# Stack rows six partitions apart, a reordered start-up, and expert weights spread over seven samples

## The chip, the cores and the metric

One core of a Trainium2 chip. The metric is the device time of one launch in microseconds (us). TensorE is PE, VectorE is DVE, ScalarE is ACT, GpSimd is POOL, SyncE is SP. SPq, ACTq and POOLq are the same engines where they issue DMAs.

## What is computed

Sixteen samples of 333 rows x 256 columns (256 image rows, 77 text rows) go through one attention block and one mixture-of-experts block. Cut to what matters:

```python
h = concat([clip(|diagonal difference| + |anti-diagonal difference|, 0, 1), table[x_txt]])   # 16 x 333 x 256
n = layernorm(h); q, k, v = n@Wq+bq, n@Wk+bk, n@Wv+bv                  # 16 heads of 16 columns
# windows of 128 rows, stride 64, and one last window: 5 windows a sample
scores = q_win @ k_win.T / 4 + pos_bias; o = softmax(scores) @ v_win    # added up, divided by the count
h = h + (merged @ Wo + bo)
# feed-forward: top 2 of 8 experts by softmax(layernorm(h) @ gate_w.T), each silu(x@w1)*(x@w3)@w2
h = h + weighted sum of the two experts
```

## The kernel before, in words

**Two phases.** First an attention phase, a software pipeline over samples. Every engine runs `step(b)` for b = -3 to 17 (L291), and each step has 20 slots k (5 windows x 4 head groups). In step b, sample b is in attention (`att`), sample b+1 is projected to q, k and v (`proj`), sample b+2 has its layernorm (`inp`), sample b+3 has its image differences (`pre`), sample b-1 is finished (`tail`) and sample b-2 is sorted to its experts (`tail2`). Then an expert phase: 91 tiles of 128 gathered rows, all on PE (L1206 to L1245).

**The order of work is written out by hand.** Each engine executes its own program in order and waits on semaphores; a DMA queue's issue order is the order of the code of SP, ACT or POOL. Nothing is planned or reordered by a tool.

**q and k in three bf16 parts.** To compute float32-like scores in bf16, q and k are split into three parts: part 0 is a bf16 copy (DVE, L757), the rest is formed on POOL (L508), part 1 is a bf16 copy of the rest (DVE, L764), part 2 what is left (POOL, L516). Scores need six products of parts, and each head has 16 columns, so the contraction is stacked to 6 x 16 = 96 rows. `Q_SLOTS = (0, 1, 2, 0, 1, 0)` and `K_SLOTS = (0, 0, 0, 1, 1, 2)` say which part stands in which of the six slots. The parts reach this layout through DRAM: SP writes each part (`write_part`, L363, two DMAs of 83.2 KB each) and loads it back once for each slot that uses it (`load_stack`, L369, one DMA of 166.5 KB for each slot, 16 partitions of 333 x 16 bf16 values). Per sample that is 12 write DMAs and 12 load DMAs. Slot s takes partitions 16s to 16s+15. PE waits for all 12 loads at the first slot of the sample (`stack_in`, L1061) and contracts over partitions 0 to 95 (L1066).

**SP's order in a step** (L334 to L403): the image loads of sample b+3 and its text indices, the positional bias in step -1 (L351, 1 MB), then for sample b+1 the writes and loads of parts mixed with each other, each load behind a wait for the write of its part (`parts_out`, L370), then the shifted copies of v (L397 to L401). The weights (`load_weights`, L317) go out in step -2.

**POOL's start-up** (L442 to L470): memsets of the image buffers, constants (`const_set` counts them to 11), both `h_in` buffers, all of `v_all` (3840 columns), the pad rows, and two DMAs of pad rows. Then its steps: the gather of the text rows in slot 0 of step b for sample b+2 (L536), the differences in slot 12 or 15 (L567), the inverse roots in slot 13 (L482 to L491), the residual in slot 18 (L598).

**DVE** waits for `zeroed` (L725) before its steps. In a step it does the max over scores plus bias (L783), the layernorm sums (L730), the normalisation (L738), the absolute values of the differences (L902), and in step 0 the negation of the bias (L750), which the first L783 needs.

**ACT** waits for `prep_done` (L629), which DVE sets when it has scaled `bq_col` (L747), and starts with the copy of xT (L639). In step 0 it issues the w1 and w3 of experts 0 to 6 in slots 2, 4, ... 14 (L668 to L672), 14 DMAs of 512 KB. The weights of expert 7 and all w2 come after the last sample (L408 to L417), since their place is used by other buffers until then.

Of the kernel before, what the change touches and what calls it, by code (L numbers as in the profile page):

```python
# [18 lines left out]
ACT = mybir.ActivationFunctionType  # L19
AX = mybir.AxisListType  # L20

P = 128
B, IMG, D = 16, 256, 256
TXT = 77
# [35 lines left out]
def build(nc, x, x_txt, table, Wq, bq, Wk, bk, Wv, bv, Wo, bo, pos_bias, gate_wT, w1, w2, w3, use, out):  # L60
    ctx = ExitStack()
    with ctx:
# [133 lines left out]
        zeroed = sem("zeroed")  # L196
        x_zeroed = sem("x_zeroed")
# [32 lines left out]
        pv_done = sem("pv_done")  # L230
        raw_ready = sem("raw_ready")
# [84 lines left out]
        def _(sp):  # L316
# [17 lines left out]
            def step(b, par):  # L334
                att, tail, tail2, proj, inp, pre = has(b)
                b0, b1, b3 = b - 1, b + 1, b + 3
                if b == -2:
                    load_weights()
                if pre:
# [10 lines left out]
                if b == -1:  # L350
                    sp.dma_start(nbias[:, :, :], pos_bias.rearrange("h q k -> q h k")).then_inc(bias_in, 16)  # L351
# [8 lines left out]
                if proj:  # L360
# [32 lines left out]
                    load_stack(1, 2, k_stack[par1], K_SLOTS)  # L393
                    vt = v_win[par1]
# [46 lines left out]
        def _(pool):  # L441
            pool.memset(x_here[:, :, :], 0.0).then_inc(x_zeroed, 1)  # L442
            pool.memset(x_below[:, :, :], 0.0).then_inc(x_zeroed, 1)
            pool.memset(text_idx[:, :], 0).then_inc(x_zeroed, 1)
            pool.memset(ident[:, :], 0.0).then_inc(const_set, 1)
# [23 lines left out]
            pool.dma_start(slots_dram[E * REGION:E * REGION + P, :], pad_rows[:, :]).then_inc(pads_in, 16)  # L469
            pool.dma_start(out[TOKENS:TOKENS + P, :], pad_rows[:, 0:D]).then_inc(pads_in, 16)  # L470
# [21 lines left out]

            def step(b, par):
                att, tail, tail2, proj, inp, pre = has(b)
                b9, b0, b1, b2, b3 = b - 2, b - 1, b + 1, b + 2, b + 3

# [22 lines left out]
                for k in range(G):  # L519
# [11 lines left out]
                    if inp and k == 0:  # L531
                        pool.wait_ge(idx_in, b2 * 16 + 16)
                        if b2 >= 2:
                            pool.wait_ge(res_ready, b2 - 1)
                            pool.wait_ge(xn_ready, b2 * 3 - 3)
                        pool.indirect_dma_start(h_in[par][0:TXT, 2, :], None, table,  # L536
                                                bass.IndirectOffsetOnAxis(text_idx[0:TXT, 0:1], 0)).then_inc(text_in, 16)
# [90 lines left out]
        def _(act):  # L628
            act.wait_ge(prep_done, 1)  # L629

            def step(b, par):
                att, tail, tail2, proj, inp, pre = has(b)
                b9, b0, b1 = b - 2, b - 1, b + 1
                for k in range(G):
# [33 lines left out]
                    if b == 0 and k >= 2 and k % 2 == 0 and k // 2 < E:  # L668

                        e = k // 2 - 1  # L670
                        act.dma_start(w1_sb[:, e], w1[e].rearrange("(c p) n -> p c n", p=P)).then_inc(expert_weights_in, 16)
                        act.dma_start(w3_sb[:, e], w3[e].rearrange("(c p) n -> p c n", p=P)).then_inc(expert_weights_in, 16)  # L672
# [41 lines left out]
        def _(dve):  # L714
# [10 lines left out]
            dve.wait_ge(zeroed, 5)  # L725
# [15 lines left out]
            def step(b, par):  # L741
# [33 lines left out]
                for k in range(G):  # L775
# [59 lines left out]
                    if tail2 and k == 3:  # L835

                        dve.wait_ge(score_e_ready, b9 + 1)
                        if b9 >= 1:
# [59 lines left out]
                    if pre and k == (13 if b > -2 else 17):  # L898
# [4 lines left out]
                    if proj and k == 14:  # L903
# [379 lines left out]
```

## Time and profile before

| | |
|---|---|
| median of 3 runs | 1293.54 us (1292.12 to 1294.58) |
| the profiled execution | 1295.08 us, span 1293.2 us |
| PE, DVE, ACT, POOL busy | 89%, 65%, 55%, 46% of the span |
| DMA | 123.31 MB, mean 95 GB/s |

The page gives busy shares over the whole span, which mixes a start-up, the attention phase (to about 750 us) and the expert phase. The view by stretches of time separates them, and the view of waits says what ended the idle time of an engine. The rows are further down.

### The profile page before, as it was taken

Reading aid. Unit: us, or ns where it says so; the run is one execution under the profiler, and the core shown is the slowest. Engines: PE = TensorE matmul, PEld = TensorE weight load, DVE = VectorE, ACT = ScalarE, POOL = GpSimd, SP = SyncE. Lnnn points to the kernel's source line nnn. Section 1 sums busy time; section 2 is a strip of 40 time slices with the busy share of each in tenths; the row PEclk is TensorE's granted clock in tenths of the full one; section 3 lists DMA queues with packets and bytes.
Section 4 is the critical chain, followed back from the end, with each engine's and each line's share of the span. In section 5 each row is a group of like instructions: output and inputs, shape, how many; then the busy total and the mean of one; then the engine's idle time right before and its main releaser. Section 6 shows DMA issues by size and latency. Waiting matters only on the chain. (4 is left out here: it accounts for less than half of the span.)

```text
span 1293.2 us, 34357 instructions
## 1 busy us (share of the span) xinstructions
PE 1154.7 (89%) x10510; PEld 950.5 (73%) x10511; DVE 839.2 (65%) x4259; ACT 707.9 (55%) x1976; POOL 595.2 (46%) x750
## 2 busy tenths in 40 slices
PE   1385999999999999999998729999999999999996
PEld 0263767666676676666766419999999999999995
DVE  4372999899899998989887643444444444444442
ACT  0194999999999999999998601111111111111110
POOL 6551576566665676656653432332223332223332
PEclk9697999999999999999998859999999999999998
DMA  3794665457554675556642171223323223323322
GB/s 103 159 254 108 133 130 116 109 134 153 123 110 108 141 157 109 109 120 130 141 95 67 35 244 29 48 48 49 49 45 49 46 48 49 49 45 49 49 46 32
DMA packets 98394, 123.31 MB, mean 95 GB/s; under 512 B 15544, under 2 KB 87416, under 8 KB 95192
## 3 DMA queue, kind: packets, MB, share of 16 engines
q1 hardware_dynamic: 75880, 89.96, 30.8%
q0 software_dynamic: 18576, 24.47, 11.8%
q10 hardware_dynamic: 3808, 7.34, 2.0%
q8 instruction: 59, 0.97, 0.4%
q14 instruction: 71, 0.58, 0.2%
HBM read 69.35 MB, written 46.07 MB: 89 GB/s over the span
## 5 line engine op out<-in xcount | busy, mean ns | idle before, releaser
L666 ACT ACTIVATE probs<-probs,neg_max 128x128 f32<-128x128 f32 x1280 | 402.3, 397 | 1.9 <-DVE neg_max L783 1.5
L783 DVE CUSTOM_DVE_ANT_0 probs<-s_bank,nbias 128x128 f32<-128x128 f32 x1280 | 293.9, 285 | 87.4 <-PE s_bank L1066 80.5
L705 ACT ACTIVATE v_all<-s_bank 128x512 f32<-128x512 f32 x91 | 54.4, 598 | 285.9 <-PE s_bank L1222 265.9
L1077 PE MATMUL t_bank<-ident,probs 128*128 128x128 f32 x1280 | 195.8, 276 | 0.2 <-ACT probs L666 0.2
L1237 PE MATMUL o_bank<-stacks,v_all 128*128 x728 | 172.4, 380 | 0.3 <-issue 0.2
L659 ACT ACTIVATE probsT<-t_bank 128x512 f32<-128x512 f32 x240 | 142.2, 592 | 42.1 <-PE t_bank L1077 40.1
L618 POOL DMA_INDIRECT out_dram<-wq_sb,nbias x46 | 75.8, 1649 | 193.2 <-DVE wq_sb L987 179.9
L1066 PE MATMUL s_bank<-stacks 96*128 96x128 bf16 x1280 | 127.3, 222 | 37.9 <-DMA stacks<-qk_parts 37.8
L1066 PEld LDWEIGHTS s_bank<-stacks 96*128 96x128 bf16 x1280 | 94.5, 99 | 82.0 <-DMA stacks<-qk_parts 40.1
L618 POOL DMA_INDIRECT out_dram<-wk_sb,nbias x45 | 73.5, 1634 | 175.8 <-DVE wk_sb L987 172.8
L993 DVE TENSOR_TENSOR v_all<-v_all,t_bank 128x512 f32<-128x512 f32 x91 | 62.6, 688 | 129.8 <-PE t_bank L1222 129.8
L1237 PEld LDWEIGHTS o_bank<-stacks,v_all 128*128 128x128 f32 x728 | 131.3, 190 | 15.1 <-issue 0.9
L1093 PE MATMUL o_bank<-probsT,v_all 128*32 128x128 f32 x2560 | 137.0, 286 | 5.8 <-ACT probsT L659 3.4
L1077 PEld LDWEIGHTS t_bank<-ident,probs 128*128 128x128 f32 x1280 | 135.9, 142 | 0.9 <-ACT probs L666 0.5
L499 POOL DMA_INDIRECT expert_slots<-rows,slot_i x96 | 97.2, 1012 | 45.2 <-issue 36.7
L699 ACT ACTIVATE v_all<-m_bank 128x256 f32<-128x256 f32 x91 | 35.0, 384 | 143.6 <-PE m_bank L1211 143.6
L783 DVE DVE_READ_ACCUMULATOR2_ANT neg_max<- 128x1 f32 x1280 | 104.8, 82 | 0.0
L1093 PEld LDWEIGHTS o_bank<-probsT,v_all 128*32 128x32 f32 x2560 | 50.5, 108 | 61.8 <-issue 47.0
L1222 PEld LDWEIGHTS s_bank<-v_all,probs 128*128 128x128 f32 x736 | 91.0, 195 | 3.2 <-ACT v_all L699 0.9
L1222 PE MATMUL s_bank<-v_all,probs 128*128 128x128 f32 x736 | 91.4, 278 | 0.5 <-ACT v_all L699 0.5
L1222 PE MATMUL t_bank<-v_all,probs 128*128 128x128 f32 x736 | 90.4, 276 | 0.0
L1222 PEld LDWEIGHTS s_bank<-v_all,parts_flat 128*128 128x128 f32 x720 | 87.4, 192 | 3.0 <-ACT v_all L699 0.7
(159 smaller groups left out, 2002.3 us busy)
## 6 DMA issues: line engine op xcount, KB each, us to landing
stacks<-qk_parts SPq DMA_DIRECT2D x192, 166.5 KB
qk_parts<-parts_flat SPq DMA_DIRECT2D x192, 83.2 KB
nbias<-expert_slots SPq DMA_DIRECT2D x91, 129.0 KB
w_sb<-in_L_ffn_w_dram ACTq DMA_DIRECT2D x14, 512.0 KB
v_all<-v_all SPq DMA_DIRECT2D x64, 96.0 KB
x_here<-in_x_dram SPq DMA_DIRECT2D x16, 256.0 KB
out_dram<-h_res SPq DMA_DIRECT2D x16, 256.0 KB
stacks<-in_L_ffn_w_dram SPq DMA_DIRECT2D x8, 512.0 KB
```

What stands on the lines that cost most here:

```text
L499: pool.indirect_dma_start(slots_dram[:, :], bass.IndirectOffsetOnAxis(slot_i[0:n, kk, j:j + 1], 0), rows[0:n, kk, j, :], None).then_inc(sc ...
L618: pool.indirect_dma_start(out[:, :], bass.IndirectOffsetOnAxis(g_rows[r][:, D + 1:D + 2].bitcast(I32), 0), y_sb[r], None, compute_op=ALU.a ...
L659: act.activation(probsT[:, r, :], t_bank[:, r, :], ACT.Copy).then_inc(pT_by_act, 1)
L666: ins = act.activation(seg, seg, ACT.Exp, bias=neg_max[:, r, i:i + 1], scale=-1.0)
L705: act.activation(hidT[r % 2], s_bank[:, r % 2, :], ACT.Silu).then_inc(silu_ready, 1)
L783: ins = dve.tensor_tensor_reduce(probs[:, r, i * WIN:(i + 1) * WIN], s_bank[:, k % 2, i * WIN:(i + 1) * WIN], nbias[:, h, :], 1.0, BIG, AL ...
L993: dve.tensor_tensor(hidT[r % 2], hidT[r % 2], t_bank[:, r % 2, :], ALU.mult).then_inc(hid_ready, 1)
L1066: mm = pe.matmul(s_bank[:, k % 2, i * WIN:(i + 1) * WIN], q_stack[par][0:KROWS, h, lo:lo + WIN], k_stack[par][0:KROWS, h, lo:lo + WIN], st ...
L1077: mm = pe.transpose(t_bank[:, (k - 3) % 2, i * WIN:(i + 1) * WIN], probs[:, r, i * WIN:(i + 1) * WIN], ident[:, :])
L1093: mm = pe.matmul(o_bank[32 * i:32 * i + 32, vp, g * WIN:(g + 1) * WIN], v_win[bp][:, w, c0:c0 + 2 * HD], probsT[:, (k - 4) % 2, i * WIN:(i ...
L1222: mm = pe.matmul(bank[:, par, n * P:(n + 1) * P], up_w[par][:, m, a, n * P:(n + 1) * P], gxT[par][:, a * P:(a + 1) * P], start=(a == 0), s ...
L1237: mm = pe.matmul(o_bank[:, r % 2, 0:D], hidT[r % 2][:, a * P:(a + 1) * P], w2_sb[:, bass.ds(e, 1), a, :].rearrange("p o n -> p (o n)"), st ...
```

## The change

It does six things.

1. `load_stack` writes slot s to partitions s, s+6, s+12, ... s+90 in place of 16s to 16s+15, for q and k alike. PE still contracts over partitions 0 to 95 of both, so each row of q still meets its row of k.
2. For sample 0 alone, SP's order is another: all writes but for two waits stand ahead of most loads.
3. The positional bias is loaded in step -2, behind the weights, in place of step -1.
4. POOL's start-up is cut up: `h_in` is zeroed first; `v_all` is filled in two halves, in steps -3 and -1; the pad rows come in slot 10 of step -1; the text gather of sample 0 goes to slot 0 of step -3. The differences of sample 1 go to slot 17 of step -2 and wait for the normalised rows of sample 0.
5. ACT runs one Exp on a constant before it waits for `prep_done`.
6. ACT issues w1[b] in slot 0 and w3[b] in slot 2 of each step b from 0 to 6, one expert for each step.

```diff
 SP, step b:
                 if b == -2:
                     load_weights()
+                    sp.dma_start(nbias[:, :, :], pos_bias.rearrange("h q k -> q h k")).then_inc(bias_in, 16)
...
-                if b == -1:
-                    sp.dma_start(nbias[:, :, :], pos_bias.rearrange("h q k -> q h k")).then_inc(bias_in, 16)
...
-                                sp.dma_start(dst[s * HD:(s + 1) * HD, :, :], parts_dram[n, part, :, :, :])\
+                                sp.dma_start(dst[s:KROWS:len(slots), :, :], parts_dram[n, part, :, :, :])\
                                     .then_inc(stack_in, 16)
-                    if b1 >= 1:
-                        sp.wait_ge(stack_in, b1 * STACK_IN)
+                    if b1 == 0:
+                        write_part(0, 0, part1_ready)
+                        write_part(1, 0, part1_ready)
+                        write_part(0, 1, part2_ready)
+                        load_stack(0, 0, q_stack[par1], Q_SLOTS)
+                        write_part(0, 2, part3_ready)
+                        write_part(1, 1, part2_ready)
+                        write_part(1, 2, part3_ready)
+                        load_stack(1, 0, k_stack[par1], K_SLOTS)
+                        for t in range(1, 3):
+                            load_stack(0, t, q_stack[par1], Q_SLOTS)
+                            load_stack(1, t, k_stack[par1], K_SLOTS)
+                if proj and b1 >= 1:
+                    sp.wait_ge(stack_in, b1 * STACK_IN)
 (the order of L378 to L393 stays for b1 >= 1)
 POOL:
+            for i in range(2):
+                pool.memset(h_in[i][:, :, :], 0.0).then_inc(h_zeroed, 1)
             pool.memset(ident[:, :], 0.0).then_inc(const_set, 1)
...
-            for i in range(2):
-                pool.memset(h_in[i][:, :, :], 0.0).then_inc(zeroed, 1)
-            pool.memset(v_all[:, :], 1.0).then_inc(zeroed, 1)
-            pool.memset(pad_rows[:, 0:D + 1], 0.0).then_inc(zeroed, 1)
-            pool.memset(rows[:, :, :, D:ROW], 0.0).then_inc(zeroed, 1)
-            pool.wait_ge(zeroed, 5)
-            pool.wait_ge(const2_set, 5)
-            (and the two DMAs of pad rows)
+            def fill_values(half):
+                n = NW * VCOLS
+                pool.memset(v_all[:, half * n:(half + 1) * n], 1.0).then_inc(v_filled, 1)
+            def fill_pads():
+                (the two memsets, wait_ge(zeroed, 2), wait_ge(const2_set, 5), the two DMAs)
...
+                    if b == -3 and k == 0:
+                        fill_values(0)
+                        pool.wait_ge(h_zeroed, 2)
+                        pool.wait_ge(idx_in, 16)
+                        gather(0)
+                    if b == -1 and k == 1:
+                        fill_values(1)
+                    if b == -1 and k == 10:
+                        fill_pads()
-                    if inp and k == 0:
+                    if inp and b2 >= 1 and k == 0:
...
-                    if pre and k == (12 if b > -2 else 15):
+                    if pre and k == (17 if b == -2 else 12):
                         pool.wait_ge(x_in, b3 * 64 + 64)
+                        if b == -2:
+                            pool.wait_ge(xn_ready, 3)
 ACT:
+            act.wait_ge(const_set, 11)
+            act.activation(raw[:, 0:P], ident[:, :], ACT.Exp).then_inc(table_loaded, 1)
+            act.wait_ge(table_loaded, 1)
             act.wait_ge(prep_done, 1)
...
-                    if b == 0 and k >= 2 and k % 2 == 0 and k // 2 < E:
-                        e = k // 2 - 1
-                        act.dma_start(w1_sb[:, e], ...); act.dma_start(w3_sb[:, e], ...)
+                    if 0 <= b < E - 1 and k in (0, 2):
+                        dst, src = ((w1_sb, w1), (w3_sb, w3))[k // 2]
+                        act.dma_start(dst[:, b], src[b].rearrange("(c p) n -> p c n", p=P)).then_inc(expert_weights_in, 16)
 DVE:
-            dve.wait_ge(zeroed, 5)
...
+                        if b9 == 0:
+                            dve.wait_ge(zeroed, 2)          (tail2, k == 3)
-                    if pre and k == (13 if b > -2 else 17):
+                    if pre and k == (17 if b == -2 else 13):
...
                     if proj and k == 14:
+                        if b1 == 0:
+                            dve.wait_ge(v_filled, 2)
```

## Rows read from the trace of the kernel before

**Rows 1.** Busy time by stretch: us, each engine (x instructions), PEclk, DMA share, GB/s.
```profile
40.00:60.00 20.00, 0.73 (x4) 0.30 (x2) 5.32 (x10) 0.00 (x0) 14.26 (x24) 0.63 0.87 155
...
100.00:120.00 20.00, 7.63 (x64) 5.86 (x65) 3.86 (x29) 5.00 (x14) 0.00 (x0) 0.58 0.55 122
120.00:140.00 20.00, 20.00 (x201) 13.91 (x200) 16.11 (x106) 18.56 (x55) 10.47 (x10) 1.00 0.43 77
...
200.00:240.00 40.00, 38.29 (x407) 27.70 (x410) 35.80 (x232) 37.46 (x111) 26.86 (x37) 1.00 0.57 129
...
840.00:880.00 40.00, 40.00 (x303) 38.43 (x302) 17.95 (x29) 7.26 (x15) 11.36 (x7) 1.00 0.32 50
```

**Rows 2.** PE timeline: start, us, line, out<-in, count [idle before, releaser].
```profile
26.58 1.34 PE L1122 MATMUL m_bank<-ident,xn 128*128 128x128 f32 x6 [26.58 <-DVE xn L738]
...
60.36 0.61 PE L1066 MATMUL s_bank<-stacks 96*128 96x128 bf16 x4 [19.63 <-DMA stacks<-qk_parts]
...
94.99 0.43 PE L1093 MATMUL o_bank<-probsT,v_all 128*32 128x128 f32 x8 [0.25 <-DVE probsT L792]
112.37 0.61 PE L1066 MATMUL s_bank<-stacks 96*128 96x128 bf16 x4 [16.96 <-DMA stacks<-qk_parts]
```

**Rows 3.** PE's waits between 200 and 700 us: us in total, times, longest.
```profile
PE m_bank L1179 <- DVE v_all L771: 7.7, 10, 1.0
...
PE s_bank L1066 <- DMA stacks<-qk_parts: 1.2, 2, 0.7
```

**Rows 4.** POOL timeline, start-up.
```profile
4.93 3.29 POOL L464 MEMSET v_all<- 128x3840 f32 x1
...
10.73 1.09 POOL L567 TENSOR_TENSOR diag<-x_here,x_below 128x512 f32<-128x512 f32 x1
...
15.75 1.07 POOL L536 DMA_INDIRECT h_in<-in_L_txt_weight_dram,text_idx  x1 [0.21 <-issue]
```

**Rows 5.** DVE timeline, start-up and first scores.
```profile
18.58 1.08 DVE L730 BATCH_NORM_STATS2 stats<-h_in 128x6 f32<-128x256 f32 x3 [5.08 <-DMA h_in<-in_L_txt_weight_dram,text_idx]
...
23.86 2.57 DVE L738 TENSOR_SCALAR xn<-h_in,moments,rstd 128x256 f32<-128x256 f32 x3 [3.99 <-POOL rstd L490]
...
50.97 1.22 DVE L750 TENSOR_SCALAR nbias<-nbias 128x2048 f32<-128x2048 f32 x1
61.13 0.29 DVE L783 CUSTOM_DVE_ANT_0 probs<-s_bank,nbias 128x128 f32<-128x128 f32 x1 [8.94 <-PE s_bank L1066]
```

**Rows 6.** ACT timeline, start-up.
```profile
28.02 1.28 ACT L639 ACT_TABLE_LOAD   x1 [28.02 <-PE m_bank L1122]
```

**Rows 7.** SP's issue timeline for sample 0.
```profile
36.04 3.64 SPq L366 DMA_DIRECT2D qk_parts<-parts_flat  x4
...
54.40 2.57 SPq L373 DMA_DIRECT2D stacks<-qk_parts  x3
```

**Rows 8.** DMA view, 42 to 43 us: packets by size; queue: packets, MB, share of 16 engines.
```profile
DMA packets 34, 0.18 MB, mean 181 GB/s; under 512 B 17, under 2 KB 17, under 8 KB 17
...
q1 hardware_dynamic: 34, 0.18, 121.8%
```

**Rows 9.** DMA view, 54 to 55 us (part writes alone, 666-byte packets).
```profile
q1 hardware_dynamic: 189, 0.12, 52.6%
```

**Rows 10.** DMA view, 66 to 67 us (ACT's weight loads, 2 KB packets).
```profile
DMA packets 197, 0.37 MB, mean 371 GB/s; under 512 B 16, under 2 KB 16, under 8 KB 197
```

**Rows 11.** SP's issue timeline for sample 1 (69 to 109 us).
```profile
76.29 2.37 SPq L373 DMA_DIRECT2D stacks<-qk_parts  x3
...
106.72 1.82 SPq L373 DMA_DIRECT2D stacks<-qk_parts  x3
```

**Rows 12.** SP's issue timeline for sample 2 (124 to 150 us).
```profile
132.23 1.35 SPq L373 DMA_DIRECT2D stacks<-qk_parts  x3
...
147.17 2.21 SPq L373 DMA_DIRECT2D stacks<-qk_parts  x3
```

**Rows 13.** DMA view, 85 to 90 us: ACT's queue, q10.
```profile
q10 hardware_dynamic: 611, 1.18, 82.8%
```

More of the change, by code:

```diff
@@ L196, in build @@
         zeroed = sem("zeroed")
+        h_zeroed = sem("h_zeroed")
+        v_filled = sem("v_filled")
         x_zeroed = sem("x_zeroed")
@@ L230, in build @@
         pv_done = sem("pv_done")
+        table_loaded = sem("table_loaded")
         raw_ready = sem("raw_ready")
@@ L393, in step @@
                     load_stack(1, 2, k_stack[par1], K_SLOTS)
+                if proj:
                     vt = v_win[par1]
@@ L461, in _ @@
                                base=TXT, pattern=[[0, 1]], channel_multiplier=-1).then_inc(const_set, 1)
-            for i in range(2):
-                pool.memset(h_in[i][:, :, :], 0.0).then_inc(zeroed, 1)
-            pool.memset(v_all[:, :], 1.0).then_inc(zeroed, 1)
-            pool.memset(pad_rows[:, 0:D + 1], 0.0).then_inc(zeroed, 1)
-            pool.memset(rows[:, :, :, D:ROW], 0.0).then_inc(zeroed, 1)
-            pool.wait_ge(zeroed, 5)
-            pool.wait_ge(const2_set, 5)
-            pool.dma_start(slots_dram[E * REGION:E * REGION + P, :], pad_rows[:, :]).then_inc(pads_in, 16)
-            pool.dma_start(out[TOKENS:TOKENS + P, :], pad_rows[:, 0:D]).then_inc(pads_in, 16)
             NEWTON = 3
@@ L491, in inverse_roots @@
                     ins.then_inc(root_step if i < NEWTON - 1 else rstd_ready, 1)
+            def fill_values(half):
+                n = NW * VCOLS
+                pool.memset(v_all[:, half * n:(half + 1) * n], 1.0).then_inc(v_filled, 1)
+            def fill_pads():
+                pool.memset(pad_rows[:, 0:D + 1], 0.0).then_inc(zeroed, 1)
+                pool.memset(rows[:, :, :, D:ROW], 0.0).then_inc(zeroed, 1)
+                pool.wait_ge(zeroed, 2)
+                pool.wait_ge(const2_set, 5)
+                pool.dma_start(slots_dram[E * REGION:E * REGION + P, :], pad_rows[:, :]).then_inc(pads_in, 16)
+                pool.dma_start(out[TOKENS:TOKENS + P, :], pad_rows[:, 0:D]).then_inc(pads_in, 16)
             def step(b, par):
@@ L495, in step, with gather @@
                 b9, b0, b1, b2, b3 = b - 2, b - 1, b + 1, b + 2, b + 3
+                def gather(n):
+                    pool.indirect_dma_start(h_in[n % 2][0:TXT, 2, :], None, table,
+                                            bass.IndirectOffsetOnAxis(text_idx[0:TXT, 0:1], 0)).then_inc(text_in, 16)
                 def scatter(kk, j):
@@ L535, in step @@
                             pool.wait_ge(xn_ready, b2 * 3 - 3)
-                        pool.indirect_dma_start(h_in[par][0:TXT, 2, :], None, table,
-                                                bass.IndirectOffsetOnAxis(text_idx[0:TXT, 0:1], 0)).then_inc(text_in, 16)
+                        gather(b2)
                     if att and k == 3:
@@ L667, in step @@
                         ins.then_inc(exp_ready, 1)
-                    if b == 0 and k >= 2 and k % 2 == 0 and k // 2 < E:
-                        e = k // 2 - 1
-                        act.dma_start(w1_sb[:, e], w1[e].rearrange("(c p) n -> p c n", p=P)).then_inc(expert_weights_in, 16)
-                        act.dma_start(w3_sb[:, e], w3[e].rearrange("(c p) n -> p c n", p=P)).then_inc(expert_weights_in, 16)
+                    if 0 <= b < E - 1 and k in (0, 2):
+                        dst, src = ((w1_sb, w1), (w3_sb, w3))[k // 2]
+                        act.dma_start(dst[:, b], src[b].rearrange("(c p) n -> p c n", p=P)).then_inc(expert_weights_in, 16)
                     v = (k - 4) // NG
@@ L837, in step @@
                         dve.wait_ge(score_e_ready, b9 + 1)
+                        if b9 == 0:
+                            dve.wait_ge(zeroed, 2)
                         if b9 >= 1:
```

## The prediction, made before the changed kernel was run

> **What bounds the kernel now.** I read the time by stretches first [rows 1]. From 200 us on, PE is busy 38.3 of 40 us, and in the expert phase 40 of 40, while DMA stands at 0.57 and 0.32. In two early stretches PE is nearly idle: 0.73 of 20 us from 40 to 60, and 7.6 of 20 from 100 to 120. So the kernel is bound by PE from about 112 us to its end, and what lies ahead of that is latency. PE's timeline names the holes [rows 2]. PE starts at 26.58, when the first normalised rows are there. Sample 0's scores start at 60.36 after 19.63 us of waiting for the stack loads. Sample 1's start at 112.37 after 16.96 us of the same wait, though PE had done sample 0's attention by 95.4. Between 200 and 700 us the same wait totals 1.2 us [rows 3]; PE's largest wait there, 7.7 us for v, is not touched by the change. Nothing behind 112 us is tied to a date of its own: samples follow each other (SP's first writes at 165.39, 206.56, 247.67: 41.1 us), then the tiles. Whatever the start gives back moves the end by as much.
>
> So there are three places: the path to PE's first work, the stack loads of sample 0, and those of sample 1.
>
> **Part 1, the path to the first work (POOL, ACT; changes 4 and 5).** Before, POOL fills all of v_all in 3.29 us, zeroes and writes the pads, and so reaches the first difference at 10.73 with no wait ahead of it; the text gather comes behind the image work, at 15.75, and DVE's sums wait 5.08 us for it, until 18.58 [rows 4, 5]. After, half the fill (1.65 us) and the gather's issue (1.07 us) stand ahead of the difference; a half fill and the pads leave. POOL's constants end at 3.64 before and at 5.1 with the two h_in memsets ahead of them. 5.1 + 1.65 + 1.07 makes 7.8, with some wait for the indices 8.1. From difference to clipped image took 4.8 us (10.73 to 15.54), so the image is there at 12.9; the gather, issued at about 7.1 and landing in 3 to 5 us, is no longer last. The sums start at 12.9 in place of 18.58, 5.7 us earlier. Sums 1.3 and roots 3.95 us keep their length. The normalisation took 2.57 us, since its first piece ran beside POOL's next difference; that difference now waits for it, so I take 3 x 0.405 less overlap, 1.1 us, from the later normalisations of the same form. The normalised rows come at 19.3 in place of 26.5. Behind that wait on POOL stand only the two differences of sample 1, and behind these DVE's absolute values and the scaling of bq_col, for which ACT waits: 19.5 + 2.1 + 0.4 + 0.2, so 22.3, 1.6 us later than PE's transposes end. ACT then copies xT without its table load of 1.28 us [rows 6]. xT is ready at 23.1 in place of 30.04: **7.0 us earlier**. The bias DMA, which stands ahead of sample 1's image on SP's queue, moves 1 MB; at the 0.37 MB for each us of [rows 10] that is 2.8 us, and puts that image at 19 to 20, about when it is asked for. If it is 2 us later, this term is 5.
>
> The second half fill and the pads (1.65 and some 1.8 us of POOL) lie in step -1. The first stands while PE projects q. The pads delay sample 1's layernorm, not sample 0's parts. Counted at nothing; without the cover the second would show in the next part.
>
> **Part 2, sample 0's stacks (changes 1, 2, 3).** Before, the first write goes out at 36.04, the last three loads from 54.40 to 56.97, and PE starts at 60.36 [rows 7]: 24.3 us. How much of that is data? Between 42 and 43 us 17 large packets of 10.7 KB (one row of a stack load) took 121.8% of 16 engine-us [rows 8]: 19.5 / 17 = 1.15 us each, 9 GB/s an engine. Each load puts one packet on each of 16 engines, so 12 loads are 13.8 us. A write is 8 packets an engine; 189 of them took 52.6% of 16 us [rows 9], 0.0445 us each, so 0.36 us. From the first large packet at 41.0 to the last at 58.3 that is 12 loads and 8 writes, 16.7 of 17.3 us. So this stretch was bound by DMA engines, and a mere reordering of SP's queue gains little.
>
> What a row six partitions further costs, no row shows. Bounds: 1.15 us again (sixteen neighbours or not is all the same), and at best the rate of the 2 KB packets, 371 / 16 = 23 GB/s, so 0.46 us [rows 10]. I take 0.6, near the fast end, since both sorts go from DRAM to SBUF over the same engines, and what sets the slow one apart is that all its rows land in sixteen neighbouring partitions. Worse than 1.15 isn't excluded and is a rival below.
> By the Trainium skill (SBUF — State Buffer, section Door 1: The DMA port swizzle) sixteen adjacent partitions reach four of 16 ports, and port use limits a DMA. Six apart, at most two rows of a load share a port, by which the packet would take half, an estimate of 0.57 us; the slow packets agree with it, and no row here tests the rest.
> Against it, the same page (The DMA setup-cost knee) has each DMA pay about 2 us whatever its size. Were that all, loads of 166.5 KB would gain nothing from their rows and the sum would be that of the first rival.
>
> Now the chain. With the parts 7.0 us earlier, part 0 of q is ready at 29.0, and part 2 of k, the last, at 36.6. SP: writes from 29.05, the last write ends at 38.8, the last load's issue at 42.6 (0.42 us each, and a wait for the last write of 2.5 us). At 0.6 us a packet the engines keep up with the issue: 42.6 + 1.05 to the first byte + 0.6 + 2.05 (58.3 to 60.36) is 46.3. At 1.15 us the data starts at 35 and takes 15.9 us: 52.9. The next to be late is DVE: sample 1's differences (POOL, 38.4, behind the pads), roots to 44.8, normalisation, then the bias at 45.9 to 47.1 (before 50.97 to 52.2, [rows 5]). So the first L783 runs at 47.6 in place of 61.13: **13.5 us earlier** (7.5 at the slow bound), part 1 included. The early bias also takes 1 MB out of the queue ahead of the first writes; that is in the 2.5 us of landing assumed here.
>
> **Part 3, sample 1's stacks (changes 1 and 6).** PE needed 35.0 us for sample 0 (60.36 to 95.4). The first three loads went out 15.9 us after its start, the last ones at 106.72, 30.4 us later [rows 11]; for sample 2 the same stretch was 14.9 us [rows 12]. The difference is ACT's seven experts: from 85 to 90 us its queue took 82.8% of the engines [rows 13], and each load waits for the landing of a write behind them. With one expert at slots 0 and 2, 1 MB, gone by about 6 us after the start, while the first write comes at 8.8 us, sample 1 has sample 2's chain: 15.9 + 14.9 + 2.2 for the last issues + 3.4 to land is 36.4 at the old packet, 1.4 beyond PE; with the faster packet each of the four waits for a write is over 1 us shorter, about 32, within PE's 35.0. The stall of 16.96 us goes: **17.0 us** (15.5 at the slow bound). The scores right after it took 0.61 us for four [rows 2] where those at full clock take 0.39; this cost of restarting PE, 0.58 of full clock in that stretch [rows 1], lasts for a few groups, 1 us at most, and I don't count it.
>
> **Part 4, the rest.** Six steps get two ACT DMA issues of 0.4 to 0.5 us; in step 0 fourteen such issues left ACT's activations back to back, nothing. Their 1 MB meets a stretch in which DMA stood at 0.43 [rows 1]. Faster packets in later samples free DMA, not PE. The expert phase is as before.
>
> **Sum.** 13.5 + 17.0 = 30.5 us. The span goes from 1293.2 to 1262.7, the profiled execution from 1295.08 to 1264.6. That execution is 1.5 us above the median, so the median goes to **1263.0**.
>
> **Rivals.** (a) *Rows make no difference to a packet.* Then 7.5 + 15.5 = 23 us, 1270.5. For it: DMA may be limited at the DRAM side or by latency. Against: the same engines carry 2.5 times as much in other transfers. It is also the case in which change 1 doesn't do what it says. 0.25. (b) *The spread weights meet stack loads that are just in time.* PE already waits for stacks twice, 1.2 us in all, between 200 and 700 us [rows 3], so some steps have no slack at the old packet. If 2.8 us of weights push the chain in each, 6 x 2.8 = 17 us comes back: 1280. Against: they are issued 12 us ahead of the first write. 0.07. (c) *Slower than before: rows six apart make each packet dearer.* It would be the stack loads of all samples. Since they are just in time, x us more for each of 12 loads costs 12x in each of 15 samples, 180x. From x = 0.17 (the 30.5 us above) it decides; at 1.5 us a packet, x = 0.35, it is 63 us on top of a start worth 23, 1333. Nothing in the trace speaks for it but that the shape doesn't occur. 0.03. The forecast's own case has 0.62; 0.03 is left for start-up waits that I haven't seen, to 1290.
>
> **How the numbers follow.** Forecast case: 1256 to 1268 from the packet at 0.46 to 0.8 and the part 1 term at 5 to 8.5. Adding (a) with 4 us for its own spread gives 1255 to 1275, which leaves (b), (c) and the remainder out, and a little of each side. A measurement tells 0.2%, 2.6 us, from no change. Faster by more: forecast, (a), (b) and most of the rest, 0.95. Within: 0.02. Slower: 0.03.
>
> **What the profile will show.** Right: PE's first transposes at 19 to 20; first L783 near 47.6; no wait for stacks at sample 1, whose scores start near 82; large packets near 0.6 us and DMA share from 200 us at 0.45 in place of 0.57; the step still 41.1 us. The forecast is wrong if the stack wait stays at either place over 3 us, if packets stay at 1.15 (then a), if steps 1 to 6 are longer than steps 8 to 13 (then b), or if all are (then c).

## The result and the profile after

The kernel takes **1264.09 us** (1263.12 to 1266.19), against 1294.06 us (1292.12 to 1296.04) for the kernel before in the same comparison. The ratio is 0.9771 [0.975, 0.9791], so 30.0 us or 2.3% faster. The forecast was 1263.0, for a gain of 30.5. The profiled execution took 1263.12 us, with a span of 1261.2 us against 1293.2.

The view by stretches comes first, in the columns of [rows 1] (stretch, length, then busy us of PE, PEld, DVE, ACT and POOL, the granted clock, DMA share, GB/s):

```profile
40.00:60.00 20.00, 10.09 (x71) 7.46 (x72) 10.03 (x58) 8.20 (x24) 11.05 (x21) 0.65 0.67 173
...
100.00:120.00 20.00, 19.68 (x209) 14.26 (x207) 19.36 (x119) 18.24 (x55) 12.48 (x23) 1.00 0.58 164
200.00:240.00 40.00, 38.77 (x412) 27.79 (x411) 36.38 (x234) 37.55 (x111) 25.99 (x35) 1.00 0.51 147
400.00:440.00 40.00, 38.77 (x413) 27.84 (x415) 36.51 (x236) 37.50 (x111) 25.78 (x37) 1.00 0.45 126
```

The second hole is gone: from 100 to 120 us PE is busy 19.68 us where it had 7.6. The first is shorter: 10.09 of the 20 us from 40 to 60, where it had 0.73. The steady stretches have the same PE work with less DMA time beside it. PE's timeline after (start, us, work, idle time before it and its releaser) answers to [rows 2]:

```profile
19.73 1.34 PE L1161 MATMUL m_bank<-ident,xn 128*128 128x128 f32 x6 [19.73 <-DVE xn L773]
...
49.91 0.61 PE L1105 MATMUL s_bank<-stacks 96*128 96x128 bf16 x4 [16.59 <-DMA stacks<-qk_parts]
...
84.38 0.40 PE L1105 MATMUL s_bank<-stacks 96*128 96x128 bf16 x4
```

Transposes start at 19.73 (26.58 before), sample 0's scores at 49.91 (60.36). The row at 84.38 is the first of sample 1's scores (112.37), and nothing stands in its brackets: no wait. PE's waits over 0 to 200 us name the stack loads once, where the view of before had both holes:

```profile
PE s_bank L1105 <- DMA stacks<-qk_parts: 16.6, 1, 16.6
```

To divide the gain I read three marks in each trace: the first scores of sample 0, SP's first write of a part for sample 2, and the first expert tile.

| mark, us | before | after | earlier by | gained since the mark above |
|---|---|---|---|---|
| first scores, sample 0 | 60.36 | 49.91 | 10.45 | 10.45, start-up and first stacks |
| first write, sample 2 | 124.47 | 95.57 | 28.90 | 18.45, the hole ahead of sample 1 |
| first expert tile | 772.85 | 740.96 | 31.89 | 3.0, steps between |
| span | 1293.2 | 1261.2 | 32.0 | 0.1, expert phase |

The forecast had 13.5, 17.0 and nothing.

**The start-up** came as the steps had it. POOL's timeline after, beside [rows 4]:

```profile
7.21 1.17 POOL L518 DMA_INDIRECT h_in<-in_L_txt_weight_dram,text_idx  x1 [0.59 <-issue]
8.42 1.09 POOL L601 TENSOR_TENSOR diag<-x_here,x_below 128x512 f32<-128x512 f32 x1
```
DVE's timeline after, beside [rows 5]:
```profile
13.26 1.08 DVE L765 BATCH_NORM_STATS2 stats<-h_in 128x6 f32<-128x256 f32 x3 [2.08 <-POOL h_in L642]
18.52 1.06 DVE L773 TENSOR_SCALAR xn<-h_in,moments,rstd 128x256 f32<-128x256 f32 x3 [3.97 <-POOL rstd L498]
```
ACT's timeline after, beside [rows 6]; ACTq is its DMA queue:
```profile
22.63 0.73 ACT L676 ACTIVATE xT<-m_bank 128x666 f32<-128x666 f32 x1 [17.29 <-DVE bq_col L782]
29.88 0.45 ACTq L708 DMA_DIRECT2D w_sb<-in_L_ffn_w_dram  x1
```

Gather issued at 7.21 (forecast 7.1), sums at 13.26 and released by the image (12.9), normalisation 1.06 us (1.1). xT's copy starts at 22.63 and ends at 23.36 (23.1), and its brackets name bq_col, as said: the forecast had PE's transposes done 1.6 us before it. The last row, the first load of expert weights, is one that the forecast put at sample 0's start, 18 us too late; it comes up again below.

**The loads** are where the forecast was off. SP's timeline after, beside [rows 7, 11]:

```profile
28.74 4.87 SPq L368 DMA_DIRECT2D qk_parts<-parts_flat  x6
33.76 1.86 SPq L375 DMA_DIRECT2D stacks<-qk_parts  x3
35.66 3.79 SPq L368 DMA_DIRECT2D qk_parts<-parts_flat  x6
39.50 6.01 SPq L375 DMA_DIRECT2D stacks<-qk_parts  x9
65.31 1.81 SPq L375 DMA_DIRECT2D stacks<-qk_parts  x3
...
78.10 2.62 SPq L375 DMA_DIRECT2D stacks<-qk_parts  x3
```

Three loads take 1.86 us of SP, nine take 6.01: 0.62 to 0.67 us each, where the working had 0.42. The nine don't stop for a write to land. By the trace's semaphore events k's last write landed at 44.10 us, 4.7 us after its issue had ended (39.45), where the working had 2.5. The DMA view from 44 to 45 us (packets by size; then the queue's packets, MB and share of 16 engines) gives the packet as [rows 8] did:

```profile
DMA packets 56, 0.30 MB, mean 298 GB/s; under 512 B 28, under 2 KB 28, under 8 KB 28
...
q1 hardware_dynamic: 56, 0.30, 122.0%
```

56 less 28 small ones leaves 28 large packets in 1.22 x 16 = 19.5 engine-us: **0.70 us a packet, where it was 1.15** and the forecast had 0.6. One microsecond is a small sample, less than two packets an engine, each counted whole where it starts, so the share can pass 100%. The 192 large packets of all twelve loads of sample 0 take 0.97 us on average before and 0.70 after. So 0.70 stands, and 1.15 was high for the stretch as a whole. Over the whole span SP's queue took 30.8% of the engines before, by the page's list of queues:

```profile
q1 hardware_dynamic: 75880, 89.96, 30.8%
```

and takes 25.4% after, with the same packets and bytes:

```profile
q1 hardware_dynamic: 75880, 89.96, 25.4%
```

### The profile page after: what moved, and what is told of

The parts are those of the page before. It is cut to its first block and busy times, and to the rows that moved or that the text cites. A ratio compares the mean times of both kernels' runs of the same rounds, so it can differ in the third digit from the quotient of the medians.

```text
span 1261.2 us, 34362 instructions
## 1 busy us (share of the span) xinstructions
PE 1149.9 (91%) x10510; PEld 946.9 (75%) x10511; DVE 837.0 (66%) x4259; ACT 706.7 (56%) x1977; POOL 594.6 (47%) x751
## 3 DMA queue, kind: packets, MB, share of 16 engines
q1 hardware_dynamic: 75880, 89.96, 25.4%
```

## The experiments

The theory from here on: three things gave the 30 us (the start-up, the packet's price, and the weights leaving the way of sample 1), each its own share. One rival is that one of them does it all and hides the others. Another, for the packet, is that the distance of the rows as such makes it cheap, or something else of the reordered code.

### Rows back in blocks of sixteen, the rest as after

```
-                                sp.dma_start(dst[s:KROWS:len(slots), :, :], parts_dram[n, part, :, :, :])\
+                                sp.dma_start(dst[s * HD:(s + 1) * HD, :, :], parts_dram[n, part, :, :, :])\
```

> The changed kernel with the stack rows back in blocks of sixteen, nothing else undone. Mine: large packets at 1.1 to 1.2 us instead of 0.70; sample 0's scores start at 52 to 55 us instead of 49.9; a wait of 0 to 2 us for stacks at sample 1, small waits at some later samples, and where one of these lets PE's clock fall, 2 us more. Median 1267 to 1273. Rival (the row spacing is worth nothing, reordering and spreading did it all): packets at 0.7 us, 1263 to 1265.

Measured: 1274.16 us (1271.68 to 1276.94), ratio to before 0.9849 [0.9811, 0.9886]. The kernel as changed is 10.1 us below it. This is rival (a) run as a kernel. The rival said 1270.5; the expectation above, 1267 to 1273 with scores at 52 to 55, missed both by 1 and 3 us. PE's timeline:

```profile
57.55 0.61 PE L1105 MATMUL s_bank<-stacks 96*128 96x128 bf16 x4 [23.63 <-DMA stacks<-qk_parts]
...
94.13 0.40 PE L1105 MATMUL s_bank<-stacks 96*128 96x128 bf16 x4 [1.83 <-DMA stacks<-qk_parts]
```

With blocks sample 0 starts at 57.55, 7.6 us later than with rows six apart, and sample 1 still waits 1.83 us (rival (a) had 52.9 and 1.4). So the new order without the cheap packet gains little at sample 0, and the packet's price counts there more than I had worked out. SP's waits from 28 to 47 us name one that the changed kernel doesn't have, for the landing of a write:

```profile
SPq L375 <- DMA qk_parts<-parts_flat: 3.0, 1, 3.0
```

The four executions stand in two pairs, 1271.7 and 1271.8 us at a mean granted clock of 0.971 to 0.972, and 1276.6 and 1276.9 at 0.967 and 0.968. The profiled one is of the first pair, 8.6 us above the changed kernel's profiled one. So part of the 10.1 us is a loss that comes and goes, and it goes with a lower clock.

### The stride alone, on the kernel before

```
-                                sp.dma_start(dst[s * HD:(s + 1) * HD, :, :], parts_dram[n, part, :, :, :])\
+                                sp.dma_start(dst[s:KROWS:len(slots), :, :], parts_dram[n, part, :, :, :])\
```

> The kernel before with the stack rows six apart, nothing else. Mine: packets at 0.70 us; sample 0's scores 3 to 6 us earlier than 60.4; the wait before sample 1 shrinks from 17.0 by 4 to 9 us, since ACT's weight loads still crowd the queue; no wait for stacks later, PE at full clock through sample 15. Median 1278 to 1286. Rival (spacing worth nothing alone): 1292 to 1295.

Measured: 1279.49 us (1278.62 to 1281.04), 0.9886 [0.9853, 0.9919]: 15.1 us for one line of code.

```profile
56.76 0.61 PE L1066 MATMUL s_bank<-stacks 96*128 96x128 bf16 x4 [15.54 <-DMA stacks<-qk_parts]
...
100.86 0.61 PE L1066 MATMUL s_bank<-stacks 96*128 96x128 bf16 x4 [8.43 <-DMA stacks<-qk_parts]
```

The two waits fall from 19.63 and 16.96 us to 15.54 and 8.43. Half of sample 1's hole closes with ACT's weights still in the way.

### The expert weights back in step 0, the rest as after

```
-                    if 0 <= b < E - 1 and k in (0, 2):
+                    if b == 0 and k >= 2 and k % 2 == 0 and k // 2 < E:
...
-                        dst, src = ((w1_sb, w1), (w3_sb, w3))[k // 2]
-                        act.dma_start(dst[:, b], src[b].rearrange("(c p) n -> p c n", p=P)).then_inc(expert_weights_in, 16)
+                        e = k // 2 - 1
+                        act.dma_start(w1_sb[:, e], w1[e].rearrange("(c p) n -> p c n", p=P)).then_inc(expert_weights_in, 16)
+                        act.dma_start(w3_sb[:, e], w3[e].rearrange("(c p) n -> p c n", p=P)).then_inc(expert_weights_in, 16)
```

> The changed kernel with ACT's fourteen weight loads back in step 0. Mine: with the faster packets the stall before sample 1 comes back in part, 7 to 13 us of its 17.0. Median 1271 to 1277. Rival (the row spacing alone had removed that stall): 1264 to 1266.

Measured: 1274.51 us (1273.61 to 1276.24), 0.9849 [0.9817, 0.9882], 10.4 us above the change.

```profile
48.98 0.61 PE L1106 MATMUL s_bank<-stacks 96*128 96x128 bf16 x4 [15.95 <-DMA stacks<-qk_parts]
...
92.82 0.61 PE L1106 MATMUL s_bank<-stacks 96*128 96x128 bf16 x4 [9.13 <-DMA stacks<-qk_parts]
```

The 9.13 us are the loss. Without a weight load in slot 0 sample 0 starts at 48.98, 0.9 us before the changed kernel's 49.91, which points at the load issued at 29.88; but two executions of one kernel differ by more (below), so that price stays uncertain.

### The spread weights alone, on the kernel before

The same edit the other way round, on the kernel before.

> The kernel before with ACT's weight loads spread over steps 0 to 6, nothing else. Mine: packets stay at 1.15 us, sample 0's scores stay at 60.4, the wait before sample 1 falls from 17.0 to 1 to 3 us, small waits at later samples stay. Median 1278 to 1282. Rival (the loads' own packets, not the weights, made that stall): the wait stays over 8 us, 1286 or more.

Measured: 1279.28 us (1274.73 to 1282.12), 0.9866 [0.9841, 0.989], 16.0 us under before.

```profile
62.76 0.61 PE L1065 MATMUL s_bank<-stacks 96*128 96x128 bf16 x4 [21.53 <-DMA stacks<-qk_parts]
...
99.27 0.40 PE L1065 MATMUL s_bank<-stacks 96*128 96x128 bf16 x4 [2.11 <-DMA stacks<-qk_parts]
```

The wait at sample 1 falls from 16.96 to 2.11 us while sample 0's grows from 19.63 to 21.53, and its scores start 2.4 us later, where they were expected to stay; why isn't known. The time between sample 2's first write and the first expert tile is 648.75 us, 648.4 before: the weights, spread over six steps, cost these steps 0.4 us even at the dear packet, though PE's small waits for stacks there come to 2.3 us in place of 1.2. That refutes rival (b), which had 17 us.

### SP's old order for sample 0

```
-                    if b1 == 0:
-                        write_part(0, 0, part1_ready)
...
-                if proj and b1 >= 1:
-                    sp.wait_ge(stack_in, b1 * STACK_IN)
+                    if b1 >= 1:
+                        sp.wait_ge(stack_in, b1 * STACK_IN)
```

> The changed kernel with SP's order for sample 0 as it was. From the copy of xT to sample 0's first scores the kernel before with only the rows six apart took 27.5 us and the changed kernel 27.3, so I expect the order to be worth nothing on this path: 1263 to 1266. Rival (each load's wait for its write costs, and the new order is what saves it): sample 0's scores 3 us or more later, 1267 or more.

Measured: 1265.07 us (1263.58 to 1267.67), 0.9768 [0.9746, 0.979]. Sample 0's scores start at 51.02, 1.1 us later; the medians are 1.0 apart, with ranges that overlap. No gain of the order is resolved, and a reordering gains little, as said.

### The bias back in step -1

```
-                    sp.dma_start(nbias[:, :, :], pos_bias.rearrange("h q k -> q h k")).then_inc(bias_in, 16)
...
+                if b == -1:
+                    sp.dma_start(nbias[:, :, :], pos_bias.rearrange("h q k -> q h k")).then_inc(bias_in, 16)
```

> The changed kernel with the bias load back in step -1, in front of the part writes. If 1 MB in the queue ahead of the writes is on the path: sample 0's scores 1 to 3 us later, 1265 to 1267. If the nine loads' issue by SP (0.67 us each) sets the end anyway: 49 to 50.5 us as now and 1263 to 1265; sample 1's image, no longer behind the bias, may even bring xT 0 to 1.5 us forward.

Measured: 1267.3 us (1264.81 to 1267.64), 0.9778 [0.976, 0.9797]. SP's timeline:

```profile
28.14 0.91 SPq L354 DMA_DIRECT2D nbias<-in_L_attn_pos_bias_dram  x1
...
37.13 1.86 SPq L376 DMA_DIRECT2D stacks<-qk_parts  x3
```

The first three loads go out at 37.13 where they went at 33.76, behind a longer wait for the first write to land, and the scores start at 51.83, 1.9 us later; the median is 3.2 us higher, though the ranges touch. In the second profiled execution of the changed kernel (further down) the loads go out at 34.95 and the scores start at 51.18, and its median is 1265.55. So 1 MB ahead of the first writes delays SP's first loads, by 3.4 or 2.2 us; what of that reaches the end is 3.2 or 1.8 us by the comparison taken, and not resolved. The working had the gain inside its landing time.

### The old start-up of POOL, DVE and ACT

```
-            for i in range(2):
-                pool.memset(h_in[i][:, :, :], 0.0).then_inc(h_zeroed, 1)
...
+            pool.memset(v_all[:, :], 1.0).then_inc(zeroed, 1)
...
-                        fill_values(0)
...
-                    if pre and k == (17 if b == -2 else 12):
+                    if pre and k == (12 if b > -2 else 15):
...
-            act.activation(raw[:, 0:P], ident[:, :], ACT.Exp).then_inc(table_loaded, 1)
```

> The changed kernel without the new start-up of POOL, DVE and ACT (fills, gather, differences, Exp as before); rows, SP's order, the early bias and the spread weights stay. Mine: xT 6.5 to 7.5 us later, near 29.3 us or 1 us more since the bias now stands ahead of sample 1's image, and all behind it as much later: 1270 to 1273. Rival (something else was late next, so that only part of the 7 us reached the end): 1265 to 1269.

Measured: 1271.26 us (1270.54 to 1271.78), 0.9814 [0.9797, 0.9831]: 7.2 us above the change, with xT's copy at 31.56 and the scores at 58.36 (49.91). In the profiled executions the difference is 8.4 us. xT comes 1.3 us later than expected, 2.3 us later than in the kernel before.

The five undoings cost 7.2, 1.0, 3.2, 10.1 and 10.4 us, 31.9 together, against 30.0 for the whole. That the sum fits doesn't make the parts independent: the medians come from different comparisons, in which the changed kernel itself stood at 1264.1 and 1265.6, and the 10.1 holds the loss that comes and goes. Done alone on the kernel before, the two large ones are worth more, 15.1 and 16.0. They overlap in the hole of 16.96 us, of which the stride alone closes 8.5 and the spread weights alone 14.9. Neither hides the other whole: undoing either costs 10 us. A kernel with both undone and the rest kept wasn't run.

### What makes a packet dear

A kernel that does nothing but load: seven phases of 12 loads, each load 16 rows of 10656 B from DRAM into 16 partitions, and each phase waited for before the next. Only the distance of the partitions differs, in this order: 1, 6, 2, 3, 4, 8, 1.

```
phase(strided(1)); phase(strided(6)); phase(strided(2)); phase(strided(3)); phase(strided(4)); phase(strided(8)); phase(strided(1))
```

> No part of the computation: seven phases of twelve loads of 16 rows x 10656 bytes from DRAM, all twelve to the same partitions, with 1, 6, 2, 3, 4, 8 and again 1 partitions from row to row. If a packet's time is set by how many of the 16 rows share a port by the Trainium skill's map (4, 2, 2, 3, 2, 2, 4 at most), phases 1 and 7 are slowest, 3 apart lies between, and 2, 4, 6 and 8 apart are alike, at half the time of the first. If it is the span of partitions that counts, time falls steadily from 1 over 2, 3, 4 to 8. If the DRAM side or latency sets it, all seven are alike.

Measured: 138.7 us; the phases stand in SP's timeline. Each row begins with the first load of a phase; two or seven of its loads fall into the window read (x2 or x7), and the second column is their issue time:

```profile
27.49 0.85 SPq L38 DMA_DIRECT2D buf<-in_x_dram  x2
...
47.97 4.41 SPq L38 DMA_DIRECT2D buf<-in_x_dram  x7
...
59.99 1.15 SPq L38 DMA_DIRECT2D buf<-in_x_dram  x2
...
72.00 1.14 SPq L38 DMA_DIRECT2D buf<-in_x_dram  x2
...
90.22 1.16 SPq L38 DMA_DIRECT2D buf<-in_x_dram  x2
...
102.23 1.12 SPq L38 DMA_DIRECT2D buf<-in_x_dram  x2
...
114.21 0.79 SPq L38 DMA_DIRECT2D buf<-in_x_dram  x2
...
134.74 0.37 SPq L52 DMA_DIRECT2D out_dram<-buf  x1
```

| partitions apart | 1 | 6 | 2 | 3 | 4 | 8 | 1 |
|---|---|---|---|---|---|---|---|
| 12 loads, us | 20.5 | 12.0 | 12.0 | 18.2 | 12.0 | 12.0 | 20.5 |

Distance 2 spans 31 partitions and is as fast as distance 8, which spans 121; distance 3 spans 46 and is slow. So the span of partitions doesn't set the time, and rows need not be neighbours to be slow. The DMA views within two phases, 1 apart (32 to 34 us) and 3 apart (84 to 86 us):

```profile
q1 hardware_dynamic: 43, 0.23, 109.6%
...
q1 hardware_dynamic: 46, 0.25, 103.0%
```

22 large packets in 1.096 x 32 engine-us are 1.59 us each, 23 in 1.030 x 32 are 1.43. In the phase 6 apart (54 to 56 us) 39 took 103.9%: 0.85. Issue isn't the limit in these phases: twelve issues at 0.63 us are 7.6 of the 12.0 us.

By the Trainium skill (SBUF — State Buffer, section Door 1: The DMA port swizzle) the port follows from bits of the partition's number: four neighbours share one, and partitions 32 further return to it. From that map I count the rows of a load that fall on the busiest port: 4 for distance 1, 3 for distance 3, 2 for distances 6, 2, 4 and 8. That is the order measured, with all four cases of two at 12.0. The number of ports that a load reaches, to which the page ties the bandwidth, doesn't give this order: it is 4 for distance 1 and 13 for distance 6, but 8 for distance 3 as for 2, 4 and 8, and distance 3 took 18.2 us where those took 12.0. The busiest port doesn't give the times in proportion either: three rows cost 18.2 us and not three quarters of 20.5. By the same page's other section that the forecast weighed (the Trainium skill, SBUF — State Buffer, The DMA setup-cost knee), a DMA pays about 2 us whatever its size. Here twelve loads of one size, issued back to back, came to 1.0 us each or to 1.7 by their partitions alone, so that cost didn't set their pace.

### The changed kernel again, and three further versions

The same kernel in another comparison:

> The changed kernel once more, as the measure for the three versions beside it: 1263 to 1266.

Measured: 1265.55 us (1263.71 to 1266.86), 0.9775 [0.9759, 0.9792], with 1294.67 (1292.36 to 1297.3) for before. Sample 0's scores start at 51.18 in its profiled execution, 49.91 in the other: marks of single executions are good to some 1.3 us. The three versions ran beside it.

First, ACT waits for bq_col only where it needs it, ahead of the first q activation, so that xT no longer waits:

```
-            act.wait_ge(prep_done, 1)
...
+                        if b1 == 0 and k == 3:
+                            act.wait_ge(prep_done, 1)
```

> The changed kernel, but ACT waits for the scaled bq_col only before the first activation that uses it, not before it copies xT. xT is copied from 21.1 us, when PE's transposes end, in place of 22.6, so all behind it comes 1.5 us earlier: scores of sample 0 at 48.4, 1262 to 1264. If something else than xT is late next, nothing is gained.

Measured: **1262.69 us** (1262.6 to 1263.84), 0.9755 [0.9741, 0.977]. ACT's and PE's timelines:

```profile
21.82 0.73 ACT L674 ACTIVATE xT<-m_bank 128x666 f32<-128x666 f32 x1 [16.49 <-PE m_bank L1161]
...
49.41 0.61 PE L1105 MATMUL s_bank<-stacks 96*128 96x128 bf16 x4 [16.25 <-DMA stacks<-qk_parts]
```

xT now waits for PE's transposes and is copied 1.1 us earlier than in its companion (22.91); the scores start 1.8 us earlier, 1.1 of it so explained, and only 0.5 us earlier than in the changed kernel's other execution (49.91). Its median is the lowest of all versions; it is 2.9 us below that of the changed kernel beside it, but one comparison decides little at 0.2%: the two ranges touch by 0.1 us, and the intervals overlap.

Second, on top of it, ACT issues sample 0's six loads of k, since SP's 0.65 us a load seemed to be the limit:

```
-                        load_stack(1, 0, k_stack[par1], K_SLOTS)
...
-                            load_stack(1, t, k_stack[par1], K_SLOTS)
...
+                    if b1 == 0 and k in (8, 9, 10):
+                        t = k - 8
+                        act.wait_ge(parts_out[1][t], PART_OUT)
```

> v1 and, for sample 0 alone, the six loads of k issued by ACT, as the writes land, while SP issues those of q. If issue (0.63 to 0.67 us a load, nine in a row on SP) sets the landing of the last load, sample 0's scores start another 1.5 to 3 us earlier, 45.5 to 47 us, and the median falls to 1260 to 1262. If the DMA engines are the limit (12 packets of 0.70 us and the writes), at most 1 us.

Measured: 1265.48 us (1265.06 to 1266.04), 0.9775 [0.976, 0.9789]: no gain, a loss of 2.8 us against the first version. ACT's issues:

```profile
34.36 1.94 ACTq L694 DMA_DIRECT2D stacks<-qk_parts  x3
...
44.45 1.80 ACTq L694 DMA_DIRECT2D stacks<-qk_parts  x3
```

Three loads of k go out by 36.3. Then ACT waits for k's second write, which landed at 44.43 by the trace's semaphore events, and the other three go out from 44.45 to 46.25. SP, free sooner, sends its copies of v (from 42.8) and images ahead of these three, and the scores start at 51.82. So SP's issue alone did not set the landing of the last load. In the changed kernel an issue (0.63 to 0.67 us) and the packet that a load puts on an engine (0.70) are about equally long, and the result fits the expectation's other case, the DMA engines as the limit. It isn't a clean test of it, since the copies of v moved ahead as well.

Third, on top of both, POOL's pads move to slot 4 of step 0:

```
-                    if b == -1 and k == 10:
+                    if b == 0 and k == 4:
```

> v2 and the pad rows written in step 0 instead of step -1: their 0.26 MB leave the queue ahead of the loads and sample 1's layernorm comes 1.7 us earlier. 0 to 1 us earlier scores, 1259.5 to 1262. A small gain or none.

Measured: 1264.37 us (1263.11 to 1265.01), 0.9767 [0.9752, 0.9782], scores at 49.41 again: not better than the first version, and above its own expectation. Against the second version, on which it stands, the scores start 2.4 us earlier and the median is 1.1 us lower, with ranges that just don't touch. So the pads in the queue may cost about 1 us; the first version with the pads moved wasn't run.

## Why the prediction was right, and where its terms were off

**Part 1, the start-up, 7.0 us: right.** xT's copy starts 6.7 us earlier, every step of the path came within 0.5 us, and SP's first write went out 7.3 us earlier (36.04 to 28.74). Undone alone the start-up is worth 7.2.

**Part 2, 13.5 us: measured 10.45.** The step that failed is "the last load's issue at 42.6", with "0.42 us each, and a wait for the last write of 2.5 us". A strided load takes SP 0.62 to 0.67 us, and nine of them in a row end at 45.51. At 0.42 they would not have ended at 42.6 either, since the last one needs k's last write, which landed at 44.10, 4.7 us after its issue. From 45.51 to the first scores it is 4.4 us and not 3.7, part of it the packet of 0.70 for the 0.6 taken (0.57 by the count of ports). The packet of before was read too dear: 12 x 1.15 us and 8 writes made 16.7 of 17.3 us, where the 192 packets average 0.97 and the DMA share from 41.0 to 58.3 us was 0.89. The engines were near their limit there, not at it. Also, the forecast had step 0's weights "gone by about 6 us after the start" of sample 0, but nothing holds ACT back in slot 0 of that step: the w1 load goes out at 29.88, among the first writes of parts. Its price is at most about 1 us and not resolved. The bias, counted at nothing beyond the landing time, held SP's first loads back by 3.4 or 2.2 us when it was put back, and sample 0's start by 0.7 or 1.9 us by the execution compared. The pads, counted at nothing, may be worth 1 us by the third version. Where the forecast said DVE would set the start, DVE was early (the bias was negated at 45.54, forecast 45.9) and the loads were late.

**Part 3, 17.0 us: right, and a little short.** The wait of 16.96 us is gone whole. The other 1.5 of the 18.45 us fit PE's restart, which no run isolates. Before, by stretches, the clock stood at 0.50 (1.2 GHz) in the first 4 us after the hole, for 3.63 busy us that are some 1.8 at full clock:

```profile
112.00:116.00 4.00, 3.63 (x25) 2.92 (x26) 0.93 (x8) 2.00 (x6) 0.00 (x0) 0.50 0.66 182
```

After, in the stretch in which sample 1's scores start, it stands at 1.00:

```profile
84.00:86.00 2.00, 1.98 (x29) 1.42 (x30) 1.74 (x16) 2.00 (x7) 1.71 (x4) 1.00 0.35 72
```

The forecast named this cost, "1 us at most", and left it out.

**Part 4, nothing: measured 3.0 us.** "Faster packets in later samples free DMA, not PE" is true of most steps, but [rows 3] show two small waits for stacks, and behind one of them the clock was at half. The profiled execution of before, at sample 15's start, in PE's timeline:

```profile
687.53 0.61 PE L1066 MATMUL s_bank<-stacks 96*128 96x128 bf16 x4 [0.65 <-DMA stacks<-qk_parts]
```

and by stretches of 2 us:

```profile
684.00:686.00 2.00, 1.76 (x19) 1.75 (x20) 0.55 (x1) 1.47 (x6) 1.47 (x1) 1.00 0.84 127
686.00:688.00 2.00, 1.35 (x19) 0.91 (x18) 1.74 (x18) 1.72 (x6) 1.08 (x2) 0.73 0.55 132
688.00:690.00 2.00, 2.00 (x17) 1.28 (x16) 1.72 (x14) 1.77 (x6) 0.00 (x0) 0.50 0.00 0
...
692.00:694.00 2.00, 2.00 (x24) 1.25 (x20) 1.63 (x15) 2.00 (x7) 0.00 (x0) 0.56 0.00 0
694.00:696.00 2.00, 2.00 (x35) 1.46 (x28) 1.90 (x7) 1.84 (x7) 0.79 (x2) 1.00 0.00 0
```

PE had been busy 1.76 of 2 us from 684 to 686, then waited 0.65 us up to 687.53, and worked at half clock, 1.2 in place of 2.4 GHz, from 686.9 (686 to 687 us stood at 0.96) to 693.8. The 3.0 us come in two pieces. From sample 2's first write to sample 15's first scores it was 563.1 us before and 561.8 after; the two waits for stacks, 1.2 us in all, make up most of that 1.3. From there to the first expert tile it was 85.3 and 83.6, which leaves 1.7 us for the half clock.

What the packet has to do with it stays open. The clock fell as the wait began, so the wait can't be all that brought it down. The clock also falls where nothing waits for stacks. With the changed kernel in SP's old order PE waited 1.22 us for `raw` up to 667.86:

```profile
666.00:668.00 2.00, 0.72 (x11) 0.30 (x10) 1.97 (x17) 2.00 (x7) 0.96 (x2) 1.00 0.00 0
668.00:670.00 2.00, 2.00 (x16) 1.61 (x19) 1.12 (x11) 1.46 (x5) 1.51 (x2) 0.54 0.09 33
```

And the changed kernel with rows back in blocks had two waits of 0.3 us and half clock at 666.4 to 669.8, but needed 645.2 us between the last two marks, the changed one 645.4, before 648.4. The totals fit a loss that comes and goes (before 1291.3 to 1299.7, the stride alone 1278.6 to 1281.0, in the same comparison), but no run isolates it. The link from the dear packet to this loss is argued, not shown.

**The rivals.** (a) was tried as a kernel and gave 1274.2 for its 1270.5: the packet counts, and rows six apart made it cheaper. (b) and (c) are refuted: no wait for stacks after sample 0, and no packet dearer. The DMA share at 200 us is 0.51 where 0.45 was said, because the spread weights pass there; at 400 us it is 0.45.

Against the forecast the measured terms are 3 us short, 1.5 over and 3 over. That their sum came within 1.5 us of the span's 32.0 is in part luck.

## What to carry to other kernels

When a DMA fills few partitions with long rows, lay them out so that no three or four of them fall on one port by that count, and choose the layout by a kernel of bare loads: 12 loads took 12.0 or 20.5 us by this alone, and a contraction doesn't care about the order of its rows. Count the issue time of the new form of a DMA too (0.65 for 0.42 us here). It came out about as long as the cheaper packet (0.70), and sharing the issue between two engines then gained nothing. A bulk load that nothing holds back goes out as early as its engine can run: give it a slot behind the work that is late, not one that is merely later in the code.

## What the runs showed of the hardware that was not expected

- A load to strided partitions costs SP more to issue than one to neighbours: 0.63 us (seven in 4.41 us, 6 apart) against 0.45 (three in 1.34 us, 1 apart) in the kernel of bare loads. In the kernel itself three loads took 1.86 us with rows six apart and 1.38 in blocks, in the same order of SP.
- The same 10.7 KB packet took 1.15 us in the kernel before (0.97 over all of sample 0's loads) and 1.59 us in the kernel of bare loads, each to sixteen neighbours, and 0.70 and 0.85 us with rows six apart. One difference between the two: the bare loads of a phase all go to the same sixteen partitions, those of the kernel to six different sets. Whether that makes them dearer stays open; it wasn't tried.
- By that count of rows on the busiest port, three cost nearly as much as four (1.43 and 1.59 us a packet), two cost 0.85.
- Short waits of PE in stretches where it was not full went with a granted clock at half for 3 to 7 us: 686.9 to 693.8 us before (a wait of 0.65 us), 668.2 to 671.6 us in SP's old order (1.22 us). From sample 15's start to the first expert tile the first left 1.7 us more than in the changed kernel.
